# Two half scans of a state-space step become one instruction over two adjoining PSUM banks, and two GpSimd products wait for VectorE

## The reference

```python
def step(h, t):
    dt_t, B_t, C_t, u_t = t
    h = h * jnp.exp(dt_t[:, :, None] * A) + (dt_t * u_t)[:, :, None] * B_t[:, None, :]
    y = jnp.einsum('bds,bs->bd', h, C_t)
    return (h, y)
```

```python
M = f_s[:, :, None] * M + i_s[:, :, None] * (vt[:, :, None] * kt[:, None, :])
n = f_s * n + i_s * kt
h_raw = jnp.einsum('bij,bj->bi', M, qt)
denom = jnp.maximum(jnp.abs(jnp.einsum('bi,bi->b', n, qt))[:, None], 1e-06)
```

## Time and profile before

| What | Value |
|---|---|
| Median of 3 runs | 1122.75 us (1122.41 to 1123.51) |
| Profiled execution: its own time, and its span | 1125.62 us, 1123.8 us |
| PE busy, DVE busy | 849.2 us (76%), 807.3 us (72%) |
| ACT busy, POOL busy | 517.0 us (46%), 553.7 us (49%) |
| Scan stage, from about 545 to 1012 us | 467 us |
| Granted PE clock, mean over the span | 0.714 of full speed |

### The profile page before, as it was taken

One profiled execution on the slowest core, in us unless ns is written; L12 is line 12 of the kernel. 1 busy time (PEld: TensorE's weight loads), 2 busy tenths in 40 slices (PEclk: granted clock), 3 DMA queues, 4 the chain that ended last, 5 costly groups with the idle time before them and its releaser, 6 DMA issues.

```text
span 1123.8 us, 11525 instructions
## 1 busy us (share of the span) xinstructions
PE 849.2 (76%) x3813; PEld 357.9 (32%) x3813; DVE 807.3 (72%) x1046; ACT 517.0 (46%) x1014; POOL 553.7 (49%) x357
## 2 busy tenths in 40 slices
PE   5588045577685589798689878888788888878887
PEld 3244022365582323243112211111111111114466
DVE  0223779976563333338899999999999999994365
ACT  0137141118425266557455555555555444444621
POOL 0000646753001000001599999999999999981100
PEclk8799568668655599989555766755656656669876
DMA  9900000070010000000111101100110110000001
GB/s 224 184 1 1 0 1 0 0 164 1 1 57 1 0 1 1 1 1 19 37 26 41 32 15 36 41 24 18 41 39 13 30 41 24 17 1 1 1 15 27
DMA packets 28248, 33.08 MB, mean 29 GB/s; under 512 B 10142, under 2 KB 27550, under 8 KB 27678
## 3 DMA queue, kind: packets, MB, share of 16 engines
q1 hardware_dynamic: 28190, 32.36, 13.0%
HBM read 17.57 MB, written 1.20 MB: 17 GB/s over the span
## 4 chain that ended last, share of the span: by engine, by line
PE 34%; DVE 30%; issue 13%; ACT 10%; POOL 7%; SPq 3%; DMA 2%; DVEq 0%; ACTq 0%; POOLq 0%
DVE pair_arrays L1579 12%; DVE pair_arrays L1563 5%; ACT pair_arrays L897 4%; PE PS L750 3%; POOL pair_arrays L1243 3%; PE PS L722 3%; PE PS L576 3%; PE PS L732 2%; PE PS L842 2%; PE PS L512 2%; DMA big<-in_x 2%; DVE pair_arrays L1385 2%; PE PS L483 2%; ACT PS L897 2%; SPq L360 2%
## 5 line engine op out<-in xcount | busy, mean ns | idle before, releaser
L1243 POOL TENSOR_TENSOR pair_arrays<-pair_arrays 128x736 f32<-128x736 f32 x192 | 332.4, 1747 | 25.1 <-DVE pair_arrays L1579 24.8
L897 ACT ACTIVATE PS<-PS,A_negative 128x368 f32<-128x368 f32 x384 | 191.6, 538 | 127.8 <-PE PS L732 127.2
L1579 DVE TENSOR_TENSOR_SCAN pair_arrays<-PS,scan_carry,pair_arrays 128x368 f32<-128x368 f32 x256 | 236.5, 965 | 0.7 <-ACT PS L897 0.4
L750 PE MATMUL PS<-pair_arrays,weights 128*32 128x368 f32 x768 | 137.2, 734 | 2.2 <-POOL pair_arrays L1243 2.2
L1205 POOL TENSOR_TENSOR big<-pair_arrays 128x1104 f32<-128x1104 f32 (+15 forms) x32 | 60.5, 1910 | 154.0 <-DVE pair_arrays L1339 118.3
L1563 DVE TENSOR_TENSOR pair_arrays<-pair_arrays,PS 128x736 f32<-128x736 f32 x144 | 128.9, 895 | 8.1 <-PE PS L722 7.9
L1579 DVE TENSOR_TENSOR_SCAN pair_arrays<-PS,pair_arrays 128x368 f32<-128x368 f32 x128 | 110.4, 905 | 2.3 <-ACT PS L897 2.3
L722 PE MATMUL PS<-spread_rows,token_weights 96*128 96x368 bf16 x192 | 65.9, 437 | 37.6 <-DVE pair_arrays L1563 23.8
L1251 POOL TENSOR_TENSOR pair_arrays<-pair_arrays,token_weights 128x736 f32<-128x736 f32 x48 | 84.0, 1751 | 18.4 <-ACT token_weights L897 18.4
L722 PE MATMUL PS<-pair_arrays,token_weights 96*128 96x368 bf16 x192 | 72.3, 475 | 24.6 <-DVE pair_arrays L1563 19.1
L1264 POOL TENSOR_TENSOR pair_arrays<-big 128x368 f32<-128x368 f32 x24 | 18.8, 806 | 133.0 <-PE PS L652 133.0
(11 more groups left out here) (190 smaller groups left out, 1272.8 us busy)
## 6 DMA issues: line engine op xcount, KB each, us to landing
big<-in_x SPq DMA_DIRECT2D x8, 1024.0 KB, 21.1
big<-decay_rows SPq DMA_DIRECT2D x4, 1104.0 KB, 16.4
spread_rows<-pair_arrays SPq DMA_DIRECT2D x96, 46.0 KB, 1.9
pair_arrays<-pair_arrays SPq DMA_DIRECT2D x96, 46.0 KB, 1.9
spread_rows<-big SPq DMA_DIRECT2D x48, 46.0 KB, 1.9
pair_arrays<-big SPq DMA_DIRECT2D x48, 46.0 KB, 1.9
weights<-in_wts SPq DMA_DIRECT2D x1, 2204.0 KB, 22.3
big<-in_wexp SPq DMA_DIRECT2D x1, 1536.0 KB, 7.6
```

Of the source, the lines that this page charges most:

```text
L750: last = nc.tensor.matmul(PS[r:r + DB, seg % 2, 0:G], w("ysel")[:, (i // 2) * DB:(i // 2 + 1) * DB], hcbuf[t % NRING][:, h, :], start=Fals ...
L897: return nc.scalar.activation(o, i, fn, **kw)
L1243: nc.gpsimd.tensor_tensor(hcbuf[t % NRING], hbuf[t % NRING], c4(seg).unsqueeze(1).to_broadcast([128, 2, G]), ALU.mult).then_inc(s("hc_read ...
L1579: nc.vector.tensor_tensor_scan(hbuf[t % NRING][:, h, :], PS[:, 4 + 2 * (t % 2) + h, 0:G], bx[t % NRING][:, h, :], carry[:, a:a + 1] if k e ...
```

## The change

Three things change.

1. **One scan a step.** `scan(t)` runs over a line of 738 = 2 x 369 columns. Each half of the line begins with a column that carries the starting state: there the decay is 0 (set once, in PSUM) and `bx` holds the state to start from. The decay of the first half now ends at the last column of one bank, and that of the second half begins in the second column of the next one, so both are contiguous. DVE's order becomes: input product of t, then the whole scan of t-1. All waits that counted two scans a step count one; the scan waits for both exponentials.
2. **Carry columns.** The starting state gets into `bx` by a new ACT copy, `carry_in(t)`, in the last eight segments. Eight small memsets on DVE set up zeros ahead of the first step.
3. **Lag products.** GpSimd makes the products of the first pair at lags 0 and 1 as soon as q and k of the first pair are there, and those of the second pair only when DVE has finished the exponents (`exponents` 2).

The buffers move accordingly (`moved` and one place of `hcbuf` to another part of token_weights). The core of the diff:

```diff
-        hbuf, hcbuf, bx = ring(0), ring(1), ring(2)
+        G1 = G + 1
+        line = [[work[:, (i * NRING + c) * 2 * G1:(i * NRING + c + 1) * 2 * G1] for c in range(NRING)] for i in range(2)]
+        hline, bline = line
+        hbuf, bx = ([a.rearrange("p (h t) -> p h t", h=2)[:, :, 1:] for a in two] for two in line)
+        bfirst = [a.rearrange("p (h t) -> p h t", h=2)[:, :, 0] for a in bline]
...
+        def decay_line(t):
+            return PS[:, 4 + 2 * (t % 2):6 + 2 * (t % 2), :].rearrange("p b c -> p (b c)")[:, 512 - G1:512 + G1]
+
+        def decay_half(t, h):
+            return PS[:, 4 + 2 * (t % 2) + h, (512 - G if h == 0 else 1):(512 if h == 0 else G1)]
...
-                pe.wait_ge(s("lag_prod"), n + 1)
+                pe.wait_ge(s("lag_prod"), 3 if n == 1 else n + 1)
...
                 if t >= 2:
-                    pe.wait_ge(s("scanned"), 2 * (t - 1))
+                    pe.wait_ge(s("scanned"), t - 1)
+                elif t == 0:
+                    pe.wait_ge(s("edges_zero"), 2)
...
+            def carry_in(t):
+
+                b, i = t // NSTEP % B, t % NSTEP
+                act.wait_ge(s("carried"), t - B * NSTEP + 1)
+                act.wait_ge(s("scanned"), t - NRING + 1)
+                f(bfirst[t % NRING], carry[:, b * DS + 2 * i:b * DS + 2 * i + 2], ACT.Copy).then_inc(s("carry_put"), 1)
...
                 if 1 <= t <= CARRIED:
                     carry_on(t - 1)
+                if B * NSTEP <= t + 2 < NSEG * NSTEP:
+                    carry_in(t + 2)
...
-            pool.wait_ge(s("qkv_ev"), 3 * NGR)
-            pool.wait_ge(s("tok_ps"), 4)
-            for n in range(NL):
+            def lag_product(n):
...
+            pool.wait_ge(s("tok_ps"), 4)
+            pool.wait_ge(s("qkv_ev"), 2 * NG)
+            lag_product(0)
+            lag_product(2)
+            pool.wait_ge(s("qkv_ev"), 3 * NGR)
+            pool.wait_ge(s("exponents"), 2)
+            lag_product(1)
+            lag_product(3)
+            pool.wait_ge(s("factors"), 2)
+            nc.gpsimd.tensor_tensor(v_, v_, li, ALU.mult).then_inc(s("iv_ready"), 1)
+            for n in range(4, NL):
+                lag_product(n)
...
+            for t in range(2):
+                step(nc.vector.memset(decay_line(t)[:, 0:1], 0.0))
+                nc.vector.memset(decay_line(t)[:, G1:G1 + 1], 0.0).then_inc(s("edges_zero"), 1)
+            for c in range(NRING):
+                step(nc.vector.memset(bfirst[c], 0.0))
...
-                dve.wait_ge(s("decay"), 2 * t + h + 1)
-                a = b * DS + 2 * i + h
-                nc.vector.tensor_tensor_scan(hbuf[t % NRING][:, h, :], PS[:, 4 + 2 * (t % 2) + h, 0:G], bx[t % NRING][:, h, :],
-                                             carry[:, a:a + 1] if k else 0.0, ALU.mult, ALU.add).then_inc(s("scanned"), 1)
+                if t >= B * NSTEP:
+                    dve.wait_ge(s("carry_put"), t - B * NSTEP + 1)
+                dve.wait_ge(s("decay"), 2 * t + 2)
+                nc.vector.tensor_tensor_scan(hline[t % NRING], decay_line(t), bline[t % NRING],
+                                             0.0, ALU.mult, ALU.add).then_inc(s("scanned"), 1)
...
             for t in range(NSEG * NSTEP):
-                if t:
-                    scan_half(t - 1, 0)
                 if not shared(t):
                     input_term(t)
                 if t:
-                    scan_half(t - 1, 1)
+                    scan(t - 1)
```

More of the change, by code:

```diff
@@ L220, in pair_of @@
             return big[:, (4 * i + 2 * p) * SP:(4 * i + 2 * p + 2) * SP].rearrange("q (b t) -> q b t", b=2)
-        def ring(i):
-            n = 2 * NRING * G
-            return [work[:, i * n:(i + 1) * n].rearrange("p (c h t) -> p c h t", c=NRING, h=2)[:, c] for c in range(NRING)]
-        hbuf, hcbuf, bx = ring(0), ring(1), ring(2)
+        G1 = G + 1
[3 more added lines that the diff above has]
+        bfirst = [a.rearrange("p (h t) -> p h t", h=2)[:, :, 0] for a in bline]
+        hc0 = 2 * NRING * 2 * G1
+        hcbuf = [a.rearrange("p (h t) -> p h t", h=2)
+                 for a in [work[:, hc0 + c * 2 * G:hc0 + (c + 1) * 2 * G] for c in range(NRING - 1)] + [Wt[:, 512 + 2 * G:512 + 4 * G]]]
+        def decay_line(t):
+            return PS[:, 4 + 2 * (t % 2):6 + 2 * (t % 2), :].rearrange("p b c -> p (b c)")[:, 512 - G1:512 + G1]
+        def decay_half(t, h):
+            return PS[:, 4 + 2 * (t % 2) + h, (512 - G if h == 0 else 1):(512 if h == 0 else G1)]
         carry = sb("scan_carry", [128, B * DS])
@@ L1592, in _ @@
                 if t:
-                    scan_half(t - 1, 1)
+                    scan(t - 1)
                 if t % NSTEP == 6 and t >= NSTEP:
                     finish_y(t // NSTEP - 1)
-            for h in range(2):
-                scan_half(NSEG * NSTEP - 1, h)
+            scan(NSEG * NSTEP - 1)
             finish_y(NSEG - 1)
```

35 lines of the change are left out of this document (14 added, 21 removed).

## The result

The changed kernel takes 1143.35 us (median of 4 runs, 1140.84 to 1145.74), the kernel before beside it 1123.13 us (4 runs, 1122.41 to 1125.11). The ratio is 1.0177, with a 95% interval from 1.0150 to 1.0203: the change makes the kernel 20 us slower. The forecast was slower, 1129 us.

A forecast was written before the change was run, and what follows sets the result against it. DVE, POOL and PE were all taken as near the limit in the scan stage. Scan stage +12.4 and lag products -6.0 gave +6.4 us on the median of 1122.75: 1129 us, range 1109 to 1139.

The forecast's parts named there:

- The merged scan, 1.68, and 24 us of work less: Scan stage, DVE: one scan of 738 columns takes 1.68 us, 1.60 from start to start; DVE loses 24 us of work.
- DVE busy about 430 of 480: Sign to look for in the changed kernel's scan stage: DVE busy about 430 of 480 us, POOL still 442.
- The train, group of 9.90: PE's chain at 1.2 GHz starts 0.84 us later; a group of four steps takes 9.90 instead of 9.38 and 9.62.
- The whole stage at 1.2 GHz: Scan stage with the clock at 1.2 GHz throughout: about 489 us (467, 4 for the clock, 18).
- With the clock shares of before: 0.76 x 18.8 - 0.24 x 8 = +12.4 us: Scan stage: 18.8 us more at 1.2 GHz, 8 less at 2.4 GHz, weighted by the old clock shares, +12.4 us.
- Never up: Rival: PE waits more often for a whole scan and stays at 1.2 GHz; stage 489, total 1139 us; chance 12%.
- a granted clock far from 0.62: Sign in the scan stage: a granted clock far from 0.62 would make the forecast's size wrong.
- the group gets longer at the lower clock with the same matmuls, so PE is busy a smaller share: Argument against the faster rival, where the clock stays up some 70% of the time (1110 us, chance 25%).
- I take 447 for the stage: Scan stage at 2.4 GHz: 447 us, as POOL's work stays 442, or 48 groups of 9.2; 8 us less than before.
- Lag products, 6 us: Lag stage: DVE is held less by GpSimd's products, 13.1 - 7.1 = 6 us saved; bounds 4.5 and 8.6.
- cost nothing that I can name: Scan stage: the rings' shifted columns cost POOL and DVE nothing; bound 5% of POOL's 442 us, 22 us.
- `carry_in`, memsets: nothing: 128 ACT copies of 206 ns hidden beside PE's step pair, at most 26 us; eight DVE memsets, at most 0.5.

The follow-up runs named there:

- e4: Changed kernel with PE's order changed (sums of y before the step pair in turns 1 and 2, shared input behind it) and ACT's input copy moved: 1103.62 us.
- g1: Kernel before plus 13 small extra matmuls on PE per group of four steps: 1122.50 us.
- e1: Kernel before with only DVE's order changed, the input product ahead of both half scans: 1150.95 us.
- f1: Changed kernel plus 13 small extra matmuls on PE per group of four steps, results unused: 1101.81 us.
- f2: Changed kernel with the lag products in the order of the kernel before: 1149.48 us.
- g3: Changed kernel plus 4 small extra matmuls on PE per group of four steps: 1142.27 us.
- e2: Kernel before with only the new order of GpSimd's lag products and its waits: 1116.59 us.
- e3: Kernel before with only the state and input ring buffers moved to the new layout: 1122.88 us.

## Why the prediction was right in direction and wrong in size

- **The merged scan, 1.68, and 24 us of work less.** Right: 1682 ns. Where DVE does not wait, a group takes 8.84 (e4), against 9.01 in the first 64 steps and 9.49 after in g1: 16 x 0.17 + 32 x 0.65 = 23.5. As a sign, "DVE busy about 430 of 480" came out as 439 of 491.
- **The train, group of 9.90.** Right: 9.93, and its starts within 0.03 of the working; DVE waits 0.67 and 0.20 where 0.8 and 0.3 were worked out. e1 shows that the order alone makes it. The whole stage at 1.2 GHz was put at 489, and it took 491.5 from its first input product. Of the 2.5 more, 1.5 lie ahead of the first scan: 2.65 from the first product to it (538.41 to 541.06), before 1.15.
- **"With the clock shares of before: 0.76 x 18.8 - 0.24 x 8 = +12.4 us".** This is the step that failed. It took the clock of before as given, and the clock fell. The share of 2.4 GHz went from 24% to 2%: granted 0.51 for 0.62. So nearly the whole stage took the price of the lower clock, and the term measured +24.4 (467.1 to 491.5). f1 shows that the clock is what the rest hangs on: with it at 0.89 the same stage takes 451.6. The rival "Never up" was the right one (+22, 1139 us) and had 12%. The prediction had also named a granted clock far from 0.62 as what would make its size wrong. By the two profiled executions the kernel would end at 1140 (1122.75 + 16.9), by the medians it ends at 1143, 4 us above the range.
- **"the group gets longer at the lower clock with the same matmuls, so PE is busy a smaller share".** Not seen: PE is busy for 85% of the stage (419.6 of 491.5), before for 84%. And e1, with longer groups and 80%, kept its clock at 0.61. The clock fell where the scan was merged and PE's order left: 0.51 in the changed kernel, 0.50 in f2, 0.51 in g3. Neither the length of a group nor PE's busy share tells it apart, and why the merge lowers the clock stays open.
- **2.4 GHz side: "I take 447 for the stage".** Near, and in part by luck: from the first product f1 has 451.6 at 0.89 and e4 451.7 at 0.77. The 447 rested on POOL's 442 us as 9.2 a group. But POOL's work had become less (417.8 us in f1's whole stage), and many groups took 8.84 to 8.97. Groups at a segment's start and at the lower clock made up for it.
- **Lag products, 6 us.** Right: 6.6 in the trace, 6.5 by e2. DVE's rows are as worked out (2.45 each, the later scan 4.52), the end 154.0 against 153.5.
- **POOL "cost nothing that I can name"; output product unchanged.** Wrong and harmless: it became 7.5% shorter, through the layout (e3), and e3's time stayed.
- **`carry_in`, memsets: nothing.** The copies (pair_arrays<-scan_carry) take 0.19 to 0.21 and lie beside PE's step pair; nothing waits for them longer than that. Groups without them (the first 64 steps) and with them take 9.93 alike.

The Trainium skill (TensorE: Matmul & The Clock Gate, A second HAM failure mode: psum-queue depth-cycling) tells of a kernel whose PE idles shortly between groups of matmuls in each iteration and whose clock goes down and up again. Here it went down and stayed: the windows from 541 to 900 us all have a granted clock of 0.50. That a few more matmuls bring it back is shown by f1; what lies between the 4 of g3 and the 13 of f1 was not tried. Why the kernel before and e1 had a fifth to a quarter of the stage at 2.4 GHz, and the changed one almost none, no run shows.

## What to carry to other kernels

An engine that is busy 98% of a stage hides the chain behind it. When an edit takes work from it, work out what each other engine waits for under the new order, at the lower clock, before the gain is booked. PE's step pair waited for the whole scan of two steps ago in every version. What the merge moved is the order: the product no longer stands inside the scan, so the scan's end, which lets PE go on, comes one half scan later for the product that waits on PE. Here that release, not the work, decided; PE's list had to be reordered with it, after which the whole change was worth -19.5 us, 6.5 of them by the lag products. Where the clock is part of the sum, take it as something that the change moves: compute both ends, and do not let the shares of before stand in for a reason. Neither longer groups nor a less busy PE foretold the fall here.
